# Node stages of a four-layer graph network in spans of four blocks, and the destination rows of the softmax passes summed by TensorE

## The chip, the cores and the metric

The kernel runs on one core of a Trainium2 chip. The metric is the device time of one execution in microseconds (us). The engines are named as in the profile: PE is TensorE (PEld its weight loads), DVE VectorE, ACT ScalarE, POOL GpSimd, SP SyncE, which only issues transfers here.

## The reference, cut to what matters

There are 3125 nodes with 64 features and 103125 edges sorted by destination. Four graph layers follow each other, each as `x = layernorm(x + layer(x))`.

```python
# 1: CompGCN, twice
comp = x[src] * rel_emb[l][ridx]
x = relu(agg_f @ w_fwd[l] + agg_b @ w_bwd[l] + x @ w_loop[l])
# 2: message network
msg = sum_l relu([x[src], edge] @ w1[l] + b1[l]) @ w2[l] + b2[l]
x = relu([x, segment_sum(msg) / deg] @ upd_w1 + upd_b1) @ upd_w2 + upd_b2
# 3: embedding of a time per node, then three GAT layers with 8 heads
emb = silu(pos_embed(noise_labels) @ te_w1 + te_b1) @ te_w2 + te_b2
x = x @ init_w + init_b + emb
e = exp(leaky_relu(al_s[src] + al_d[dst]) - m[dst])
x = silu(batchnorm(segment_sum(alpha * xw[src]) + gat_b + x @ adj_w + adj_b))
x = x @ out_w + out_b
# 4: attention over the edges, with K, V, Q = x @ W + b
```

## The kernel before, in words

Nodes lie in 25 blocks of 128 (NB = 25), one node per partition. Edges lie in groups of 512 of one destination block. The program is a chain of stages; between two of them every engine meets the others (`Stage.__exit__`). Two kinds of stage alternate.

**Passes over the edges** (`compgcn_pass` twice, `message_pass`, `gat_pass` three times, `attention_pass`): 114 steps of 8 tiles of 128 edges. In each step POOL issues 8 indirect transfers (L660) that gather the source rows from a table in DRAM into a ring of four buffers; it waits until the buffer of four steps ago has been used up. `pipeline` (L584) writes each engine's program as parts with lags: a few steps written out as a head, then a loop of four steps a turn, then a tail.

In `gat_pass` a step goes round PE and DVE. DVE raises the running maximum of the two destination blocks (`maxima`, L1609 to L1638) and leaves it, with the destination terms of the logits, as three bf16 parts per group in `gat_parts`. PE looks up the destination rows of the 1024 edges (`dst_gather`, L1735): eight matmuls of 48 columns, 3 parts x 16 values side by side. DVE adds the three parts (L1644, into `gat_drow`), makes the logits (L1647 to L1653), and later the messages (L1660). PE's order in a step is `turn` (L1707), `sums(0)` (L1745), `dst_gather` (L1735), `turn_back` (L1713), `sums(1)` (L1745) and `pick` (L1723); DVE's `maxima` of the next step waits for `pick`, and `turn` for the gathered rows by way of ACT (L1566).

**Stages over the nodes**: `compgcn_nodes`, `project_nodes` (tables of the message and attention passes), `message_nodes`, `diffusion_embed`, `gat_tables`, `gat_nodes`, `diffusion_out`. Each is a hardware loop, block by block or in rounds of five blocks. In most of them DVE first copies the block into a tile with a fixed address (`flat`), PE transposes it, ACT copies the transpose out of PSUM (`tall`), PE multiplies it with the weights, and DVE or ACT writes the result; one bank is used for each of these products, and PE starts a block's transposes only when ACT has emptied the bank, its products only when the copy is there. In `compgcn_nodes`:

```python
pe.wait_ge(staged, b * 2 + 2)
pe.wait_ge(evacuated, b * 2 + 1)
pe.transpose(agg_t[:, 0:P], flat[:, 0:P], m.ident[:, :])
pe.transpose(x_t[0:DIM, 0:P], flat[:, P:3 * DIM], m.ident[:, :]).then_inc(turned, 1)
pe.wait_ge(evacuated, b * 2 + 3)
```

`diffusion_embed` computes, ahead of its loop, the angles of all 3200 nodes on DVE (L1346 to L1353) and their sine on ACT (L1368), and in its loop the two products of the time network. `gat_tables` multiplies each block with weights that hold a zero column per head, and adds the ones of these columns by a matmul with one row (L1487); its table goes to DRAM block by block (L896). `gat_nodes` waits after its loop for all blocks, then runs the statistics of the batch norm on DVE (L1808, L1810), the root on ACT (L1832) and a SiLU over the whole tile on ACT (L1835). A product in f32 stands in the trace as two matmul records and two weight loads, a transpose as one.

Of the kernel before, what the change touches and what calls it, by code (L numbers as in the profile page):

```python
# [20 lines left out]
ALU = mybir.AluOpType  # L21
# [24 lines left out]
ROUND = 5  # L46
# [7 lines left out]
def build(nc, a, out):  # L54
    m = Mem()
    m.norms = 0
    with ExitStack() as ctx:
# [45 lines left out]
        with ExitStack() as c:  # L103
# [5 lines left out]
            residual_norm(nc, m, m.y)  # L109
        message_tables(nc, m, a)  # L110
        message_pass(nc, m, a)
        message_nodes(nc, m, a)
        with ExitStack() as c:
            def cb(name, shape, dt=F32):
                return c.enter_context(nc.sbuf_tensor(name, shape, dt))
            m.ft = cb("ft", [P, 2, NP])
            m.ft2 = cb("ft2", [P, 2, NP])
            m.al_d, m.top = cb("al_d", [P, NB, HEADS]), cb("top", [P, NB, HEADS])
            m.dst_parts = cb("dst_parts", [P, NB, PARTS, HEADS], BF16)
            cur, nxt = m.ft, m.ft2  # L120
# [12 lines left out]
        finish(nc, m, out)  # L133

# [449 lines left out]
def pipeline(eng, *parts, per_turn=RING):  # L584


    last = max(lag for lag, _ in parts)
    head = -(-last // per_turn) * per_turn
    whole = STEPS // per_turn * per_turn

    def at(times):
        for t in times:
            for lag, part in parts:
                if 0 <= t - lag < STEPS:
                    part(Step(None, (t - lag) // per_turn, (t - lag) % per_turn, per_turn))

    at(range(head))
    with eng.Fori(head // per_turn, whole // per_turn) as turn:
        for r in range(per_turn):
            for lag, part in parts:  # L600
                part(Step(turn, (r - lag) // per_turn, (r - lag) % per_turn, per_turn))
    at(range(whole, STEPS + last))

# [288 lines left out]
def write_table(sp, table, tile, width, stored, ahead, written):  # L892

    with sp.Fori(0, NB) as b:
        sp.wait_ge(stored, b + (1 + ahead))
        sp.dma_start(table[ds(b * P, P), :].unsqueeze(1), tile[:, ds(b, 1), 0:width]).then_inc(written, 16)  # L896
    sp.wait_ge(written, 16 * NB)


def compgcn_nodes(nc, m, a, layer, x, y):  # L900

    with Stage(nc, f"gcn_nodes{layer}") as st:
        loaded, staged, turned = st.sem("loaded"), st.sem("staged"), st.sem("turned")
        evacuated, product, stored, written = st.sem("evacuated"), st.sem("product"), st.sem("stored"), st.sem("written")
        w_agg, w_loop = st.sb("w_agg", [P, DIM]), st.sb("w_loop", [DIM, DIM])
        first = st.sb("first", [P, 1])
        flat, tall, tall_x = st.sb("flat", [P, 3 * DIM]), st.sb("tall", [P, P]), st.sb("tall_x", [DIM, P])
        agg_t, x_t, res = m.ps[0], m.ps[1], m.ps[2]
        with nc.Block() as block:
            @block.sync  # L910
            def _(sp):
# [3 lines left out]
                if layer == 0:  # L915
                    write_table(sp, m.x_table, y, DIM, stored, 1, written)

            @block.vector
            def _(dve):
                with dve.Fori(0, NB) as b:  # L920
                    dve.wait_ge(turned, b + 1)
                    dve.tensor_copy(flat[:, 0:P].unsqueeze(1), m.acc[:, ds(b, 1), 0:P]).then_inc(staged, 1)
# [1170 lines left out]
```

## Time and profile before

| | |
|---|---|
| median of 3 runs | 9469.13 us (9462.7 to 9487.42) |
| the profiled execution | 9480.35 us |
| its span | 9478.5 us |
| PE busy | 6510.8 us (69%) |
| POOL busy | 6088.3 us (64%) |
| DVE busy | 4520.1 us (48%) |
| ACT busy | 2030.6 us (21%) |
| mean granted TensorE clock | 0.655 of full speed |

Busy times are sums over stages that are bound by different things, so they are read stage by stage. The granted clock has two levels here, 0.5 (1.2 GHz) and 1.0 (2.4 GHz); a mean between them is a mix in time.

### The profile page before, as it was taken

How to read it: one execution, taken by the hardware profiler on the slowest of the kernel's cores; microseconds unless marked ns; L12 is line 12 of the kernel's file. 1: busy time of each engine (PE TensorE's matmuls, PEld its weight loads, DVE VectorE, ACT ScalarE, POOL GpSimd, SP SyncE). 2: the span in 40 equal slices, each digit the busy share in tenths (PEclk: the TensorE clock that was granted, in tenths of full speed). 3: DMA queues.
4: the chain of work that ended last, by engine and by line, in shares of the span. 5: the costliest groups of instructions: out<-in, count | busy, mean ns of one | idle time of the engine just before them, and what ended most of it. 6: DMA issues, size and time to landing. Idle time of an engine off the chain costs nothing. (4 is left out here: it accounts for less than half of the span.)

```text
span 9478.5 us, 139096 instructions
## 1 busy us (share of the span) xinstructions
PE 6510.8 (69%) x32379; PEld 5639.1 (59%) x32380; DVE 4520.1 (48%) x12932; ACT 2030.6 (21%) x5522; POOL 6088.3 (64%) x6396
## 2 busy tenths in 40 slices
PE   3556666666655556477877777777778888666766
PEld 3555556666544444346666646666667877566666
DVE  4444423333211111347777637777746666444444
ACT  2333321111122222212222212222122222211111
POOL 4777747777467777056666446666537777277776
PEclk7666555656577777567777767777755555566666
DMA  4555533333133333045555335554424444144443
GB/s 137 167 168 171 165 86 92 93 91 91 43 92 92 91 92 83 8 128 152 149 148 148 97 108 149 149 151 147 119 69 116 115 113 115 41 137 131 131 131 104
DMA packets 780185, 1092.58 MB, mean 115 GB/s; under 512 B 395392, under 2 KB 435008, under 8 KB 779728
## 3 DMA queue, kind: packets, MB, share of 16 engines
q1 hardware_dynamic: 546352, 588.70, 20.4%
q0 software_dynamic: 233760, 503.07, 20.1%
q8 instruction: 26, 0.43, 0.0%
q14 instruction: 47, 0.39, 0.0%
HBM read 1016.16 MB, written 75.04 MB: 115 GB/s over the span
## 5 line engine op out<-in xcount | busy, mean ns | idle before, releaser
L660 POOL DMA_INDIRECT gat_rows<-xw_table,gat_index x2736 | 2592.4, 948 | 1758.6 <-issue 1075.6
L1745 PE MATMUL bank<-gat_msg_s,gat_hot 128*128 128x264 f32 (+1 forms) x5472 | 1799.6, 497 | 27.2 <-DVE gat_msg_s L1660 26.5
L1745 PEld LDWEIGHTS bank<-gat_msg_s,gat_hot 128*128 128x128 f32 x5472 | 1322.7, 283 | 267.4 <-issue 32.0
L872 PE MATMUL bank<-gcn_rel,gcn_rhot 100*128 100x64 f32 x3648 | 763.3, 397 | 867.2 <-DVE gcn_rhot L827 867.0
L872 PEld LDWEIGHTS bank<-gcn_rel,gcn_rhot 100*128 100x128 f32 x3648 | 729.7, 306 | 911.3 <-issue 455.9
L660 POOL DMA_INDIRECT att_rows<-pre_table,att_index x912 | 862.8, 946 | 448.7 <-issue 276.0
L660 POOL DMA_INDIRECT msg_rows<-pre_table,msg_index x912 | 862.6, 946 | 412.7 <-issue 277.8
L660 POOL DMA_INDIRECT gcn_rows<-x_table,gcn_index x912 | 883.7, 969 | 361.5 <-issue 277.8
L660 POOL DMA_INDIRECT gcn_rows<-in_x,gcn_index x912 | 883.0, 968 | 333.9 <-issue 270.2
L1723 PEld LDWEIGHTS bank<-gat_ends_s,gat_hot 128*128 128x128 f32 x5472 | 966.7, 267 | 34.7 <-ACT gat_hot L698 2.9
L1723 PE MATMUL bank<-gat_ends_s,gat_hot 128*128 128x9 f32 x5472 | 916.8, 305 | 3.5 <-DVE gat_ends_s L1599 2.1
L709 PE MATMUL bank<-gcn_msg_s,gcn_hot 128*128 128x128 f32 x3648 | 768.6, 397 | 17.7 <-DVE acc L720 17.7
L840 DVE TENSOR_TENSOR bank<-gcn_rows,bank 128x512 f32<-128x512 f32 x228 | 158.7, 696 | 1293.0 <-DMA gcn_rows<-x_table,gcn_index 713.3
L709 PEld LDWEIGHTS bank<-gcn_msg_s,gcn_hot 128*128 128x128 f32 x3648 | 733.0, 306 | 18.8 <-issue 18.8
L709 PE MATMUL bank<-msg_msg_s,msg_hot 128*128 128x129 f32 x1824 | 394.7, 403 | 459.6 <-ACT msg_msg_s L1131 453.2
L1660 DVE TENSOR_TENSOR gat_msg_s<-gat_rows,bank 128x2112 f32<-128x2112 f32 (+1 forms) x342 | 680.8, 1991 | 0.1
L709 PEld LDWEIGHTS bank<-msg_msg_s,msg_hot 128*128 128x128 f32 x1824 | 365.3, 306 | 485.7 <-DVE acc L720 356.2
L709 PE MATMUL bank<-att_msg_s,att_hot 128*128 128x64 f32 x1824 | 384.8, 399 | 344.3 <-DVE att_msg_s L1996 340.8
L709 PEld LDWEIGHTS bank<-att_msg_s,att_hot 128*128 128x128 f32 x1824 | 366.4, 307 | 375.0 <-ACT att_hot L698 269.3
L1146 DVE TENSOR_TENSOR msg_pre_s<-msg_rows,bank 128x512 f32<-128x512 f32 x228 | 146.5, 684 | 887.3 <-DMA msg_rows<-pre_table,msg_index 879.8
L1735 PE MATMUL bank<-gat_parts,gat_dhot 128*128 128x48 bf16 x2736 | 156.4, 206 | 512.6 <-DVE gat_parts L1638 391.4
L1735 PEld LDWEIGHTS bank<-gat_parts,gat_dhot 128*128 128x128 bf16 x2736 | 125.7, 110 | 639.3 <-issue 635.4
(300 smaller groups left out, 9118.8 us busy)
## 6 DMA issues: line engine op xcount, KB each, us to landing
gcn_ids<-rel_rows SPq DMA_DIRECT2D x228, 400.0 KB
gat_hot_half<-edge_hots SPq DMA_DIRECT2D x342, 256.0 KB
gat_dhot<-dst_hots SPq DMA_DIRECT2D x342, 256.0 KB
gcn_dst<-dst_rows SPq DMA_DIRECT2D x114, 512.0 KB, 6.7
gat_rows<-xw_table,gat_index POOLq DMA_INDIRECT x2736
edge_hots<-gcn_hot_half SPq DMA_DIRECT2D x114, 256.0 KB, 2.1
dst_hots<-gcn_dhot SPq DMA_DIRECT2D x114, 256.0 KB, 3.5
gcn_hot_half<-edge_hots SPq DMA_DIRECT2D x114, 256.0 KB
```

The source lines that it names most:

```text
L660: pool.indirect_dma_start(self.rows[n.q][:, j, :], None, self.table, bass.IndirectOffsetOnAxis(ap=self.index[n.q][:, j:j + 1], axis=0))\
L709: ins = pe.matmul(place(banks, g, width), hot[:, g * GROUP + j, :], msg[:, g * GROUP + j, 0:width], start=j == 0, stop=j == GROUP - 1)
L840: dve.tensor_tensor(comp[q], g.rows[n.q][:, :, :], rel_ps[q][:, :].rearrange("p (b d) -> p b d", b=BATCH), ALU.mult)\
L872: ins = pe.matmul(rel_ps[q][:, j * DIM:(j + 1) * DIM], rhot[q][:, j * P:(j + 1) * P], rel[:, :], start=True, stop=True)
L1146: ins = dve.tensor_tensor(pre[q][:, part, :], g.rows[n.q][:, part, :], edge_ps[q][i][:, :].rearrange("p (j d) -> p j d", j=GROUP), ALU.add)
L1660: dve.tensor_tensor(msg[q][:, :, :].rearrange("p b (h e) -> p b h e", h=HEADS), rows[n.q][:, :, 0:wide].rearrange("p b (h e) -> p b h e", ...
L1723: ins = pe.matmul(pick_ps[:, j * (HEADS + 1):(j + 1) * (HEADS + 1)], hot[n.q][:, j, :], ends[q][:, j, :], start=True, stop=True)
L1735: ins = pe.matmul(row_ps[:, j * size:(j + 1) * size], dhot[n.q][:, j * P:(j + 1) * P], parts[q][:, j // GROUP, :, :].rearrange("p k h -> p ...
L1745: ins = pe.matmul(sum_ps[g][:, 0:wide], hot[n.q][:, g * GROUP + j, :], msg[q][:, g * GROUP + j, :], start=j == 0, stop=j == GROUP - 1)
```

## The change: what it does

All node stages are written out (no hardware loop) over seven spans, six of four blocks and one of one. Each span has one of two banks (and of two SBUF tiles) in turn; PE transposes span i before it multiplies span i-1 (`in_turn`), straight from `m.acc` and `x`, without `flat`. `message_nodes` does this with three lags. Tables go to DRAM span by span.

- The time network moves out of `diffusion_embed` into the head of `message_pass`, in seven chunks of 512 nodes on DVE, ACT and PE; `pipeline` takes parts with a count, and writes 12 steps out as the head, where it wrote 4. Seven loads on SP move with it, ahead of the loads of the edge attributes. The two buffers of `turn_ps` there become one.
- `gat_tables` has no zero columns and no matmul of ones (DVE writes them into `m.acc`), eight banks instead of two, and the SiLU of the layer before, span by span; `gat_nodes` takes its statistics span by span, and multiplies `adj` with 512 columns at a time.
- In `gat_pass` PE adds the three parts in PSUM: 24 matmuls of 16 columns a step. L1644 and the tile `drow` are gone; the logits read the bank, and `dst_gather` waits for `shifted` of the step before instead of `joined`.

```diff
-ROUND = 5
+SPAN = 4
+SPANS = [(b, min(SPAN, NB - b)) for b in range(0, NB, SPAN)]
+def in_turn(first, second):
+    for i in range(len(SPANS) + 1):
+        if i < len(SPANS):
+            first(i, *SPANS[i])
+        if i:
+            second(i - 1, *SPANS[i - 1])
...
 def compgcn_nodes(nc, m, a, layer, x, y):
+                def turn(i, b, size):
+                    if i >= 2:
+                        pe.wait_ge(agg_kept, i - 1)
+                        pe.wait_ge(x_kept, i - 1)
+                    for k in range(size):
+                        pe.transpose(agg_t[i % 2][:, k * P:(k + 1) * P], m.acc[:, b + k, 0:P], m.ident[:, :])
+                    for k in range(size):
+                        ins = pe.transpose(x_t[i % 2][0:DIM, k * P:(k + 1) * P], x[:, b + k, :], m.ident[:, :])
+                    ins.then_inc(turned, 1)
+                def products(i, b, size):
+                    pe.wait_ge(agg_kept, i + 1)
+                    pe.wait_ge(x_kept, i + 1)
+                    if i >= 2:
+                        pe.wait_ge(stored, i - 1)
+                    for k in range(size):
+                        out = res[i % 2][:, k * DIM:(k + 1) * DIM]
+                        pe.matmul(out, tall[i % 2][:, k * P:(k + 1) * P], w_agg[:, :], start=True, stop=False)
+                        ins = pe.matmul(out, tall_x[i % 2][:, k * P:(k + 1) * P], w_loop[:, :], start=False, stop=True)
+                    ins.then_inc(product, 1)
...
 def message_pass(nc, m, a):
+                pipeline(act, (0, g.bring_index(act)), (5, time_keep, TIMES), (4, time_hidden, TIMES), (1, keep),
+                         (2, hot.widen(act, summed, 1)), (2, rectify), (2, wave, TIMES))
+                pipeline(dve, (0, angles, TIMES), (1, preactivations), (3, adds))
+                pipeline(pe, (0, turn), (3, time_input, TIMES), (2, sums), (0, edge_products), (3, time_output, TIMES))
...
 def gat_tables(nc, m, a, layer, cur):
+                if layer:
+                    for i, span in enumerate(SPANS):
+                        activate(act, m, layer, cur, active)(i, *span)
+                for b in range(NB):
+                    keep(b)
...
-                    pe.matmul(o_ps[q][:, 0:both], m.ones[0:1, :], one[:, :], start=False, stop=True).then_inc(product, 1)
+                        if b >= DEEP:
+                            pe.wait_ge(terms, b - DEEP + 1)
+                        for k in range(kt):
+                            ins = pe.matmul(m.ps[b % DEEP][:, 0:width + 2 * HEADS], cur[:, k, b * P:(b + 1) * P], w[:, k, :],
+                                            start=k == 0, stop=k == kt - 1)
...
 def gat_pass(nc, m, layer):
-                    dve.tensor_reduce(drow[q][:, :, :], row_ps[:, 0:BATCH * PARTS * 2 * HEADS]
-                                      .rearrange("p (b k h) -> p b h k", b=BATCH, k=PARTS), AX.X, ALU.add).then_inc(joined, 1)
-                    dve.wait_ge(joined, n.total(1, 2))
-                    dve.tensor_tensor(lg[q][:, :, :], al_s[q][:, :, :], drow[q][:, :, 0:HEADS], ALU.add)\
+                    dve.tensor_tensor(lg[q][:, :, :], al_s[q][:, :, :], drow[:, :, 0:HEADS], ALU.add)\
...
-                    pe.wait_ge(joined, n.total(1, 1))
+                    pe.wait_ge(shifted, n.total(1, 1))
                     for j in range(BATCH):
-                        ins = pe.matmul(row_ps[:, j * size:(j + 1) * size], dhot[n.q][:, j * P:(j + 1) * P],
-                                        parts[q][:, j // GROUP, :, :].rearrange("p k h -> p (k h)"), start=True, stop=True)
+                        for k in range(PARTS):
+                            ins = pe.matmul(row_ps[:, j * size:(j + 1) * size], dhot[n.q][:, j * P:(j + 1) * P],
+                                            parts[q][:, j // GROUP, k, :], start=k == 0, stop=k == PARTS - 1)
...
 def gat_nodes(nc, m, a, layer, cur, nxt):
+                for i in range(1, len(SPANS)):
+                    divide(i, *SPANS[i])
+                    measure(i - 1, *SPANS[i - 1])
```

How PE's instructions stand in the loop of the first `gat_pass`, before (`gat_hot` holds the 0/1 tiles of destinations, `gat_dhot` their transposes):

```order
L1707 MATMUL bank<-ident,gat_al_s 64x128
L1745 MATMUL bank<-gat_msg_s,gat_hot 128x264 x4
L1735 MATMUL bank<-gat_parts,gat_dhot 128x48 x8
L1713 MATMUL bank<-ident,gat_run_max 128x64
L1745 MATMUL bank<-gat_msg_s,gat_hot 128x264 x4
L1723 MATMUL bank<-gat_ends_s,gat_hot 128x9 x8
```

and now:

```order
L1794 MATMUL bank<-ident,gat_al_s 64x128
L1833 MATMUL bank<-gat_msg_s,gat_hot 128x264 x4
L1823 MATMUL bank<-gat_parts,gat_dhot 128x16 x24
L1800 MATMUL bank<-ident,gat_run_max 128x64
L1833 MATMUL bank<-gat_msg_s,gat_hot 128x264 x4
```

Sixteen matmuls more stand ahead of `turn_back`, `sums(1)` and `pick`. On DVE, in the same loop, there stood before:

```order
L1638 TENSOR_TENSOR gat_parts<-gat_rest 128x2x8
L1591 REGISTER_ALU
L1592 SCALAR_TENSOR_TENSOR gat_run_max<-gat_runs,bank 64x128
L1644 TENSOR_REDUCE gat_drow<-bank 128x128
L1647 TENSOR_TENSOR gat_lg<-gat_al_s,gat_drow 128x64
```

and now:

```order
L1728 TENSOR_TENSOR gat_parts<-gat_rest 128x2x8
L1681 REGISTER_ALU
L1682 SCALAR_TENSOR_TENSOR gat_run_max<-gat_runs,bank 64x128
L1734 TENSOR_TENSOR gat_lg<-gat_al_s,bank 128x64
L1737 SCALAR_TENSOR_TENSOR gat_lg<-gat_lg 128x64
```

The reduction between the scan and the first sum is gone. ACT in one of the steps of the head of `message_pass` now (`te_hid` is the hidden layer of the time network, `rnd` and `ang` its angles):

```order
L670 ACTIVATE msg_index<-src_i 128x8
L1187 ACTIVATE ft<-bank,msg_b_in 128x512
L1183 ACTIVATE msg_te_hid<-bank,msg_te_b 128x512
L1168 ACTIVATE msg_attr_t<-bank 128x256
L718 ACTIVATE msg_hot<-msg_hot_half 128x1024
L1174 ACTIVATE msg_msg_s<-msg_pre_s 128x8x128
L1179 ACTIVATE msg_rnd<-msg_ang 128x512
```

L1187, L1183 and L1179 are new; they stand behind the copy of the gather's indices (L670), and the other four rows were there before.

## Rows read from the trace of the kernel before

**Rows 1.** The page: span, busy times by engine, and what the DMA engines moved.
```profile
span 9478.5 us, 139096 instructions
...
PE 6510.8 (69%) x32379; PEld 5639.1 (59%) x32380; DVE 4520.1 (48%) x12932; ACT 2030.6 (21%) x5522; POOL 6088.3 (64%) x6396
...
GB/s 137 167 168 171 165 86 92 93 91 91 43 92 92 91 92 83 8 128 152 149 148 148 97 108 149 149 151 147 119 69 116 115 113 115 41 137 131 131 131 104
```

**Rows 2.** The gathers of the first and the third `gat_pass`: first and last start.
```profile
L660 POOL DMA_INDIRECT gat_rows<-xw_table,gat_index x912: 943/949/991, 4103.0 to 5367.8; - x183
...
L660 POOL DMA_INDIRECT gat_rows<-xw_table,gat_index x912: 941/947/985, 6993.8 to 8133.3; - x183
```

**Rows 3.** Windows, node loops: start:end, us, busy of PE, PEld, DVE, ACT, POOL; PEclk.
```profile
1277.00:1342.50 65.50, 48.09 (x150) 31.00 (x150) 7.92 (x48) 16.26 (x75) 0.00 (x0) 0.50 0.05 12
...
2606.20:2637.90 31.70, 19.13 (x75) 15.66 (x75) 6.50 (x15) 3.76 (x10) 0.00 (x0) 0.50 0.14 42
3803.40:3879.60 76.20, 49.18 (x170) 35.07 (x170) 12.62 (x25) 12.34 (x30) 0.00 (x0) 0.50 0.00 0
3893.20:4028.30 135.10, 59.78 (x175) 40.20 (x175) 49.29 (x112) 45.41 (x52) 0.00 (x0) 0.50 0.04 13
4035.00:4097.30 62.30, 61.54 (x100) 24.98 (x100) 5.64 (x25) 10.07 (x25) 0.00 (x0) 0.50 0.15 54
5469.00:5554.40 85.40, 84.87 (x150) 41.82 (x150) 6.89 (x25) 10.10 (x25) 0.00 (x0) 0.50 0.11 39
6935.00:6988.00 53.00, 52.73 (x150) 37.49 (x150) 6.76 (x23) 7.38 (x25) 0.00 (x0) 0.50 0.11 33
8200.00:8229.70 29.70, 16.57 (x50) 12.58 (x50) 5.62 (x25) 7.42 (x24) 0.00 (x0) 0.50 0.00 0
8249.60:8288.00 38.40, 24.46 (x75) 19.93 (x75) 8.29 (x20) 3.76 (x10) 0.00 (x0) 0.50 0.11 34
5419.00:5441.70 22.70, 22.64 (x184) 21.80 (x182) 9.35 (x22) 14.42 (x47) 0.00 (x0) 0.99 0.00 0
```

**Rows 4.** Timeline of PE in `message_nodes`: start, us, instruction, and the idle time before.
```profile
3803.47 1.33 PE L1254 MATMUL bank<-ident,msg_nodes_flat 128*128 128x128 f32 x5 [12.49 <-DVE msg_nodes_flat L1239]
3805.66 2.39 PE L1266 MATMUL bank<-msg_nodes_w,msg_nodes_tall 128*128 128x64 f32 x10 [0.85 <-ACT msg_nodes_tall L1286]
...
3811.53 2.40 PE L1272 MATMUL bank<-msg_nodes_both_t,msg_nodes_w_u 128*64 128x512 f32 x4 [0.85 <-ACT msg_nodes_both_t L1290]
```

**Rows 5.** Timeline of DVE and ACT behind the loop of the first `gat_nodes`.
```profile
5442.33 3.78 DVE L1808 BATCH_NORM_STATS2 gat_nodes_stats<-ft 128x6 f32<-128x512 f32 x7 [2.20 <-ACT ft L1825]
...
5452.48 6.00 ACT L1835 ACTIVATE ft<-ft,gat_nodes_shift,gat_nodes_gain 128x3200 f32<-128x3200 f32 x2
```

**Rows 6.** Timeline of PE: the lookup at the high clock, then a step at the low one.
```profile
4701.28 0.36 PE L1735 MATMUL bank<-gat_parts,gat_dhot 128*128 128x48 bf16 x8 [3.28 <-DVE gat_parts L1638]
...
4723.11 0.48 PE L1735 MATMUL bank<-gat_parts,gat_dhot 128*128 128x48 bf16 x8 [2.70 <-DVE gat_parts L1638]
4723.52 0.69 PE L1713 MATMUL bank<-ident,gat_run_max 64*128 64x64 f32 x2
4724.14 3.89 PE L1745 MATMUL bank<-gat_msg_s,gat_hot 128*128 128x264 f32 x8
4727.81 3.42 PE L1723 MATMUL bank<-gat_ends_s,gat_hot 128*128 128x9 f32 x16
4731.09 0.40 PE L1707 MATMUL bank<-ident,gat_al_s 128*64 128x128 f32 x1
```

**Rows 7.** Groups: busy us, mean ns, idle before, releasers (L1723: first `gat_pass` alone).
```profile
L1644 DVE TENSOR_REDUCE gat_drow<-bank 128x128 f32<-128x384 f32 x342 | 190.6, 557 | 131.2 <-PE bank L1735 122.2 <-issue 8.1
L1735 PEld LDWEIGHTS bank<-gat_parts,gat_dhot 128*128 128x128 bf16 x2736 | 125.7, 110 | 639.3 <-issue 635.4
L1723 PE MATMUL bank<-gat_ends_s,gat_hot 128*128 128x9 f32 x1824 | 274.6, 288 | 1.1 <-ACT gat_hot L698 0.7 <-DVE gat_ends_s L1599 0.4
```

**Rows 8.** Timeline of PE in `attention_pass`: 24 matmuls of 64 columns, three parts each.
```profile
8907.93 1.49 PE L2040 MATMUL bank<-q_parts,att_dhot 128*128 x24
```

More of the change, by code:

```diff
@@ L584, in pipeline @@
 def pipeline(eng, *parts, per_turn=RING):
-    last = max(lag for lag, _ in parts)
-    head = -(-last // per_turn) * per_turn
+    last = max(part[0] for part in parts)
+    early = max([part[0] + part[2] for part in parts if len(part) > 2], default=0)
+    head = -(-max(last, early) // per_turn) * per_turn
     whole = STEPS // per_turn * per_turn
@@ new lines, in products @@
+                def products(i, b, size):
+                    pe.wait_ge(kept, i + 1)
+                    if i >= 2:
+                        pe.wait_ge(stored, i - 1)
+                    for k in range(size):
+                        at = k % each * width
+                        ins = pe.matmul(res[i % 2][k // each][:, at:at + width], tall[i % 2][:, k * P:(k + 1) * P], w[:, :],
+                                        start=True, stop=True)
+                    ins.then_inc(product, 1)
+                pe.wait_ge(loaded, 32 * len(parts))
@@ L1235, in _ @@
                 dve.wait_ge(rated, 2)
[L1236 to L1247 removed]
+                staged((0, join), (2, store))
@@ new lines, in turn_joined, with hide @@
+                def turn_joined(i, b, size):
+                    pe.wait_ge(joined, i + 2)
+                    if i:
+                        pe.wait_ge(joined_kept, i)
+                    for k in range(size):
+                        ins = pe.transpose(bt_ps[:, k * P:(k + 1) * P], both[:, b + k, :], m.ident[:, :])
+                    ins.then_inc(joined_t, 1)
+                def hide(i, b, size):
+                    pe.wait_ge(joined_kept, i + 1)
+                    if i >= 2:
+                        pe.wait_ge(hidden, i - 1)
+                    pe.matmul(h_ps[i % 2][0:DIM, 0:size * P], w_u1[:, :], both_t[i % 2][:, 0:size * P], start=True, stop=True)\
+                        .then_inc(hidden_ps, 1)
@@ new lines, in _, with turn, products @@
+            @block.tensor
+            def _(pe):
+                def turn(i, b, size):
+                    if i >= 2:
+                        pe.wait_ge(kept, i - 1)
+                    for k in range(size):
+                        ins = pe.transpose(t_ps[i % 2][0:DIM, k * P:(k + 1) * P], m.x[:, b + k, :], m.ident[:, :])
+                    ins.then_inc(turned, 1)
+                def products(i, b, size):
+                    pe.wait_ge(kept, i + 1)
+                    if i >= 2:
+                        pe.wait_ge(stored, i - 1)
+                    pe.matmul(o_ps[i % 2][:, 0:size * P], w_in[:, :], tall[i % 2][:, 0:size * P], start=True, stop=True)\
+                        .then_inc(product, 1)
+                pe.wait_ge(loaded, 16)
+                in_turn(turn, products)
@@ new lines, in gat_shape, with gat_columns, activate, part @@
+def gat_shape(layer):
+    return (1, 2, 2)[layer], (256, 256, 128)[layer]
+def gat_columns(layer):
+    kt, width = gat_shape(layer)
+    c = width // HEADS
+    wide = HEADS * (c + 1)
+    return kt, c, wide, wide + HEADS, wide + 2 * HEADS
+def activate(act, m, layer, cur, counted):
+    ot = gat_shape(layer - 1)[1] // P
+    def part(i, b, size):
+        for o in range(ot):
+            tile = cur[:, o, b * P:(b + size) * P]
+            ins = act.activation(tile, tile, ACT.Silu, bias=m.shift[:, o:o + 1], scale=m.gain[:, o:o + 1])
+        ins.then_inc(counted, 1)
+    return part
```

668 lines of the change are left out of this document (320 added, 348 removed).

## Prediction

> **What bounds the kernel now.** I read the page first, then the windows on each loop, then the timelines inside them. The page [rows 1] has PE at 69%, POOL at 64% and DVE at 48%: no engine is the bound everywhere, so I go stage by stage. The profiled execution took 9480.35 us, 11.2 above the median of 9469.13; the sum is made against the first and the median's number is 11 less. Differences under 0.3%, 28 us, can't be told from no change.
>
> The passes over the edges are bound in two ways. In the first `gat_pass` 912 gathers start over 1264.8 us: 1.388 us each, 11.1 us for a step of eight; in the third they take 1.251 each, 10.0 a step [rows 2]. The second is POOL's own uninterrupted pace (a gather of 0.95 and 0.30 before the next), the first is not: there the round of DVE and PE sets the step, and POOL waits for buffers.
>
> The node loops are bound by one block's round trip. Their windows add up to 577 us, counting the loop of `compgcn_nodes`, which runs twice, once [rows 3]. In `message_nodes` PE does a block's 5 transposes in 1.33 us, idles 0.85 until ACT has copied, does ten records in 2.39, idles 0.85 again, does four in 2.40 [rows 4]. PEclk is 0.50 in all of them, the low of the clock's two levels (1.2 GHz). The `gat_nodes` loop shows the other, 0.99, right behind a pass [rows 3].
>
> **Prices at the low clock**, all from [rows 4], with 0.4 taken off for filling the array (the one transpose of [rows 6] takes 0.40): a transpose (1.33−0.4)/4 = 0.23 us; a record of 64 or 128 columns (2.39−0.4)/9 = 0.22, two to a product; of the last row's 2.40, two records of 512 columns, 0.85 each, which is 0.43 per block for a product taken over four blocks.
>
> **The node stages.** With two banks and the transposes of span i ahead of the products of span i−1, DVE's and ACT's copies (at most 16.3 us busy of 65.5 in the first window) lie beside PE, and the stage becomes PE's stream over 25 blocks plus a fill:
> - `compgcn_nodes`, twice: two transposes, four records: 25×(0.46+0.88) = 33.5, plus 1, against 65.5: −31 each, −62.
> - tables of `message_pass`: 25×(0.23+0.44) = 16.8, plus 1.9, against 31.7: −13.
> - `message_nodes`: 25×(0.46+0.88+0.43) = 44.3, plus 2, against 76.2, and it starts some 3 earlier, as nothing is copied flat: −33.
> - `diffusion_embed`: angles and sine leave it. What stays is a load (I estimate 3.6) and 25×(0.23+0.43) = 16.5, plus 2: 22 against 135.1: −113.
> - `gat_tables`: PE is busy over 98% of it [rows 3] at the low clock, on 288 or 160 columns a block and the ones' matmul. One unbroken stream of that kind is what PE had before the one loop where 0.99 was granted. I take the high clock after 4 us: the first table 62.3 → 20.4 (then 3.5 MB at 171 GB/s, the page's fastest slice, bind), −42; the second 85.4 → 27, −58; the third 53 → 17, −36: −136. At the low clock it is only the matmuls left out: −35−36−27 = −98.
> - `gat_nodes`: the statistics (7 in 3.78 us, twice, [rows 5]) lie beside the loop, −8; the 6.00 of SiLU and its switch move behind the next stage's weight work, −7; a reciprocal and a shorter start, −2: −17 twice, −10 for the last, −44.
> - `diffusion_out` 29.7 → 25×0.44+1.3 = 12.3: −17.5. Tables of `attention_pass` 38.4 → 25×(0.23+0.68)+1 = 23.8: −14.5.
>
> These are −433. Unrolling costs nothing by itself: its cover is that the written-out heads of the passes run at their loops' pace.
>
> **The time network in `message_pass`.** Seven chunks on DVE, PE and ACT, one to a step. The ring of four buffers gives POOL four steps, 40 us, before a late step stops it. ACT's three new instructions stand ahead of other work, behind the copy of the indices (order, L670), so POOL is fed first. Seven loads on SP go ahead of the edge attributes. I take 2 us, up to 20 if the head of twelve steps turns into a round as in `gat_pass`. Without the ring's slack it would be the 45 to 49 us that ACT and DVE were busy in the embed window [rows 3].
>
> **The lookup in `gat_pass`.** Removed: L1644, 0.557 us on DVE's path, 342 times; DVE idled 131.2 ahead of it, 122.2 of them for the bank, which now comes ahead of the sum at L1734 instead [rows 7]. Added: eight matmuls of 48 columns become 24 of 16. Before they take 0.36 us at the high clock and 0.48 at the low [rows 6]. Bounds for the 24: below, the same pace per matmul, (0.36−0.2)/7 = 0.023, so 0.2+23×0.023 = 0.73; above, `attention_pass`, whose 24 of 64 columns take 1.49 [rows 8]. Four times the columns are streamed there, so I lean to the near end: 0.9 at the low clock and 0.75 at the high. That is +0.42 and +0.39 on PE, and `turn_back`, `sums(1)` and `pick` stand behind it. `pick` releases DVE's scan, and a step's PE work at the low clock is full (0.69+3.89+3.42 follow without a gap, [rows 6]).
>
> `pick` averages 2.41 us in that pass, between 1.85 at the high clock and 3.42 at the low (rows 6 and 7): about 36% of the steps are low. There PE is the longer side: +0.42. In the others DVE is: −0.557 and the 0.03 that a second instruction waits to start, +0.39, so −0.2 on the round from the parts to the logits. Over 228 steps of the first two passes: 228×(0.36×0.42−0.64×0.2) = +5. In the third, POOL's pace covers most: +0.07×114 = +8. With the 2 of `message_pass`: +15. The new wait (`shifted` for `joined`) holds PE until DVE has read the bank, a sum of 64 elements just behind the old reduction's place: nothing, since PE waits 3.28 for the parts ahead of each lookup anyway.
>
> **Sum:** −433+15 = −418: 9480.35−418 = 9062 for a profiled execution, **9051** on the median.
>
> **The rivals.**
> - *A, the lookup costs what attention's does.* 1.49 for 24: +1.0 at the low clock; at the high one I take 1.15, which nets +0.2 (1.15−0.36−0.59). For: same count and same 0/1 tiles as weights. Against: 8 in 0.36 [rows 6]. First two passes 228×(0.36×1.0+0.64×0.2) = 111, third 0.65×114 = 74, in place of 13: 9223. The Trainium skill ("TensorE: Matmul & The Clock Gate", section "Back-to-back issue gap") gives matmuls of up to 64 columns a floor of 25 ns, or 62 ns with hardware decode off; 24 of them would be an estimated 0.6 or 1.49 us, and the row of 8 in 0.36 disagrees with the second. Chance 0.12.
> - *B, the denser streams keep the high clock in more node stages.* What is left of their PE time after the change, some 33.5×2+17+44+16+11+23 = 178 us, would shrink by up to 79: 8970. Against: their records are transposes and narrow f32 products, PE was at 65 to 75% in these loops and never granted more than 0.50 [rows 3]. Chance 0.10.
> - *C, slower than before: each of the 24 pays its own weight load on the path.* A load at L1735 averages 110 ns from start to end [rows 7]; 24 unhidden are 2.64 us. On the low clock +2.2, less what DVE saves where it is the longer side (0.59×0.64): +1.83×342 = +626, and 9469−433+626 = 9662. Against: the same row has 125.7 us busy over 2736 loads, 46 ns each, and 8 loads and matmuls fit in 0.36. It decides the sign from 0.087 us a matmul (24 in 2.1 us). The skill's page "TensorE: Matmul & The Clock Gate", section "LDWEIGHTS (loading the stationary operand)", makes a load columns/1.2 ns, an estimated 107 ns for these 128 and 2.57 us for 24, which speaks against this change; the row of 8 in 0.36 disagrees, as 8 would take 0.86. Chance 0.03.
> - *D, the node loops gain nothing*: PE was 65 to 75% busy in them, and written-out code could stall as it is fetched. Only the embed stage, the tables' matmuls and the batch norm then move, −113−98−44+15 = −240: 9229. Chance 0.03.
>
> **How the numbers follow.** The forecast has 0.72. In it, tables at the low clock give +38, the fill of 20 in `message_pass` +18, and shorter fills with the lookup at its lower end some −35: 9015 to 9107. To leave out no more than 2 in 10, the range takes B in, down to 8950, and reaches most of the way to A, 9200. All cases but C are faster by far more than 28 us: faster 0.96, slower 0.03, same 0.01.
>
> **What would show it.** Right: embed near 22 us; `compgcn_nodes` near 35 at PEclk 0.50 and `message_nodes` near 46; PEclk near 1 in the three tables, with the first at 150 GB/s or more; gathers still at 1.251 in `message_pass` and its end no later; L1823 x24 near 0.9; gathers of the first `gat_pass` at 1.38 to 1.40, DVE idling for the bank ahead of L1734. Wrong: L1823 at 1.4 or more (A, C), gathers of the third pass above 1.30, PEclk above 0.6 in the early node stages (B), idle "issue" between PE's matmuls in the spans (D).

## The result, and the profile after

The changed kernel takes **9018.11 us** (9012.4 to 9021.1) against 9468.91 before: a ratio of **0.952, 95% interval 0.9504 to 0.9537**. The forecast was 9051, with a range of 8950 to 9200. The profiled execution's span is 9019.3, 459.2 less than before; the forecast for it was −418.

The page of the changed kernel, its span, busy times, granted clock and what the DMA engines moved (answers to [rows 1]):

```profile
span 9019.3 us, 144258 instructions
...
PE 6468.0 (72%) x37299; PEld 5691.4 (63%) x37300; DVE 4270.9 (47%) x12350; ACT 1977.4 (22%) x5277; POOL 6074.9 (67%) x6396
...
GB/s 132 168 169 172 168 117 92 91 92 92 76 77 93 91 93 92 66 156 150 152 151 150 95 160 148 148 147 148 94 114 113 116 113 113 68 132 131 132 130 104
```

The gathers of its three gat passes, first to last start ([rows 2] has the first and third of before; its second took 1264.5 us):

```profile
L680 POOL DMA_INDIRECT gat_rows<-xw_table,gat_index x912: 940/946/995, 3823.9 to 5074.3; - x183
...
L680 POOL DMA_INDIRECT gat_rows<-xw_table,gat_index x912: 940/946/957, 5184.9 to 6456.5; - x183
...
L680 POOL DMA_INDIRECT gat_rows<-xw_table,gat_index x912: 938/944/967, 6568.9 to 7711.3; - x183
```

The first starts of all passes cut the span into passes and the node stages between them. Worked out from such rows in both traces:

| stretch | before | after | change | forecast |
|---|---|---|---|---|
| between the gcn passes | 84.7 | 52.4 | −32.3 | −31 |
| gcn to message pass | 135.9 | 98.9 | −37.0 | −31−13 |
| message pass to first gat pass | 320.8 | 115.2 | −205.6 | −33−113−42 |
| first to second gat pass | 192.6 | 110.6 | −82.0 | −17−58 |
| second to third | 168.9 | 112.4 | −56.5 | −17−36 |
| third gat pass to attention | 171.8 | 137.0 | −34.8 | −10−17.5−14.5 |
| node stages together | | | −448.2 | −433 |
| the three gat passes | 3668.8 | 3664.4 | −4.4 | +13 |
| gcn, message, attention passes | | | −6.6 | +2 |

So 448 of the 459 us lie between the passes, and the passes, nine tenths of the time, moved by 0.1%. A stretch holds more than node stages: the last gather of a pass is followed by the steps that are still to be summed, and behind the third gat pass the lookup has made this part longer (further down). Where the stages went is in the windows on their loops (columns as in [rows 3]; the row of `gat_nodes` is left out), in order: the two `compgcn_nodes`, tables of the message pass, `message_nodes`, `diffusion_embed`, the three `gat_tables`, `diffusion_out`, tables of the attention pass:

```profile
1275.10:1308.60 33.50, 33.31 (x150) 27.92 (x150) 4.38 (x7) 6.28 (x14) 0.00 (x0) 0.65 0.09 20
2485.90:2527.00 41.10, 40.91 (x150) 34.05 (x150) 4.38 (x7) 6.32 (x14) 0.00 (x0) 0.50 0.00 0
2545.70:2564.60 18.90, 18.67 (x75) 14.60 (x75) 4.08 (x7) 3.81 (x7) 0.00 (x0) 0.50 0.25 71
3726.40:3760.90 34.50, 31.20 (x164) 22.10 (x164) 10.34 (x23) 11.21 (x21) 0.00 (x0) 0.84 0.00 0
3776.60:3795.50 18.90, 18.67 (x39) 7.18 (x39) 4.01 (x6) 3.81 (x7) 0.00 (x0) 0.50 0.00 0
3802.90:3817.80 14.90, 14.68 (x50) 11.37 (x50) 4.20 (x24) 9.38 (x25) 0.00 (x0) 0.80 0.49 172
5153.00:5178.50 25.50, 25.25 (x100) 20.30 (x100) 4.19 (x24) 11.80 (x30) 0.00 (x0) 0.92 0.31 110
6547.30:6563.00 15.70, 15.41 (x100) 15.20 (x100) 4.15 (x24) 10.27 (x32) 0.00 (x0) 0.81 0.31 94
...
7775.80:7786.90 11.10, 10.93 (x50) 10.74 (x50) 2.64 (x7) 2.73 (x5) 0.00 (x0) 0.50 0.00 0
7807.60:7831.70 24.10, 24.00 (x75) 18.65 (x75) 5.81 (x12) 3.81 (x7) 0.00 (x0) 0.50 0.18 55
```

PE's busy time now fills its windows to 98% and more (90% in `message_nodes`), where it filled 44% to 73% of them before, the tables of the gat passes left aside [rows 3]: the loops have become PE's stream. The three tables run at 0.80 to 0.92 of full clock instead of 0.50, and so does, unforeseen, `message_nodes` (0.84).

In the passes the lookup takes about the same at both clocks. Timeline of PE, a step at the high clock and one at the low:

```profile
4405.62 0.79 PE L1823 MATMUL bank<-gat_parts,gat_dhot 128*128 128x16 bf16 x24 [0.24 <-issue]
...
4416.16 0.77 PE L1823 MATMUL bank<-gat_parts,gat_dhot 128*128 128x16 bf16 x24 [3.25 <-DVE gat_parts L1728]
```

What DVE saved came back as waits for PE. Groups of the first gat pass after (busy us, mean ns of one, idle before), then those that answer to L1833 and L1699 in the same pass of before:

```profile
L1833 PE MATMUL bank<-gat_msg_s,gat_hot 128*128 128x264 f32 x1760 | 669.7, 545 | 6.7 <-DVE gat_msg_s L1747 6.6
...
L1810 PE MATMUL bank<-gat_ends_s,gat_hot 128*128 128x9 f32 x1778 | 293.3, 303 | 0.8 <-DVE gat_ends_s L1689 0.8
...
L1734 DVE TENSOR_TENSOR gat_lg<-gat_al_s,bank 128x64 f32<-128x64 f32 x111 | 24.5, 221 | 79.8 <-PE bank L1823 79.8
L1699 DVE TENSOR_SCALAR gat_pen<-bank 128x8 f32<-128x8 f32 x111 | 18.4, 166 | 203.7 <-PE bank L1810 161.5 <-issue 42.3
```

```profile
L1745 PE MATMUL bank<-gat_msg_s,gat_hot 128*128 128x264 f32 x1760 | 632.8, 521 | 11.4 <-DVE gat_msg_s L1660 11.0
L1609 DVE TENSOR_SCALAR gat_pen<-bank 128x8 f32<-128x8 f32 x111 | 18.5, 167 | 190.6 <-issue 118.3 <-PE bank L1723 72.3
```

DVE no longer spends 0.557 us a step on L1644, 62 us in this pass. Ahead of the logits it now idles 79.8 us for the bank, where it idled 41.3, and ahead of `maxima` 203.7 instead of 190.6, most of it for `pick` now. That is 52 of the 62 us. PE in its turn has become slower: the same 1760 records of the message sums take 37 us longer, `pick` 24.5 longer (268.8 to 293.3) and the lookup 37.8 longer (49.2 to 87.0). The sums and the picks together are 61 us over 111 steps, 0.55 a step; in the second pass it is 0.47. What makes these two slower stands in the granted clock of the first two passes, before and after:

```profile
4103.00:5368.00 1265.00, 984.91 (x4771) 808.19 (x4771) 905.70 (x2993) 276.99 (x1126) 864.08 (x912) 0.75 0.51 151
5560.00:6825.00 1265.00, 982.17 (x4758) 805.57 (x4759) 905.89 (x2993) 276.56 (x1124) 864.04 (x912) 0.75 0.51 151
```

```profile
3824.00:5074.00 1250.00, 1076.07 (x6538) 890.33 (x6538) 842.75 (x2882) 279.62 (x1122) 861.29 (x911) 0.69 0.52 152
5185.00:6456.00 1271.00, 1065.91 (x6533) 885.98 (x6534) 840.62 (x2882) 281.20 (x1123) 860.79 (x911) 0.70 0.51 150
```

### The profile page after: what moved, and what is told of

Its sections match the earlier page's. It is cut to its first block and busy times, and to the rows that moved or that the text cites. A ratio compares the mean times of both kernels' runs of the same rounds, so it can differ in the third digit from the quotient of the medians.

```text
span 9019.3 us, 144258 instructions
## 1 busy us (share of the span) xinstructions
PE 6468.0 (72%) x37299; PEld 5691.4 (63%) x37300; DVE 4270.9 (47%) x12350; ACT 1977.4 (22%) x5277; POOL 6074.9 (67%) x6396
## 5 line engine op out<-in xcount | busy, mean ns | idle before, releaser
L680 POOL DMA_INDIRECT gat_rows<-xw_table,gat_index x2736 | 2585.1, 945 | 1417.5 <-issue 1061.9
L1833 PE MATMUL bank<-gat_msg_s,gat_hot 128*128 128x264 f32 (+1 forms) x5472 | 1868.7, 512 | 10.1 <-DVE gat_msg_s L1747 9.5
L1833 PEld LDWEIGHTS bank<-gat_msg_s,gat_hot 128*128 128x128 f32 x5472 | 1369.6, 291 | 255.5 <-issue 13.8
L1810 PEld LDWEIGHTS bank<-gat_ends_s,gat_hot 128*128 128x128 f32 x5472 | 1030.4, 282 | 40.2 <-issue 3.2
L1810 PE MATMUL bank<-gat_ends_s,gat_hot 128*128 128x9 f32 x5472 | 971.8, 316 | 2.2 <-DVE gat_ends_s L1689 2.2
L1823 PEld LDWEIGHTS bank<-gat_parts,gat_dhot 128*128 128x128 bf16 x8208 | 250.3, 102 | 609.8 <-issue 606.4
L1823 PE MATMUL bank<-gat_parts,gat_dhot 128*128 128x16 bf16 x8208 | 268.8, 173 | 475.8 <-DVE gat_parts L1728 363.0
```

The lines of the kernel that those rows point to most:

```text
L680: pool.indirect_dma_start(self.rows[n.q][:, j, :], None, self.table, bass.IndirectOffsetOnAxis(ap=self.index[n.q][:, j:j + 1], axis=0))\
L1810: ins = pe.matmul(pick_ps[:, j * (HEADS + 1):(j + 1) * (HEADS + 1)], hot[n.q][:, j, :], ends[q][:, j, :], start=True, stop=True)
L1823: ins = pe.matmul(row_ps[:, j * size:(j + 1) * size], dhot[n.q][:, j * P:(j + 1) * P], parts[q][:, j // GROUP, k, :], start=k == 0, stop=k ...
L1833: ins = pe.matmul(sum_ps[g][:, 0:wide], hot[n.q][:, g * GROUP + j, :], msg[q][:, g * GROUP + j, :], start=j == 0, stop=j == GROUP - 1)
```

## The experiments

Theory: the node stages carry the whole gain, and the lookup nothing, since DVE's and PE's rounds in a gat pass are about equally long, and the clock falls when PE has more matmuls. Rivals: the lookup gains or costs by itself; one of the two rounds alone sets the step; written-out code or spans alone, not the overlap, gained in the node stages.

The first four runs fell on a chip on which the kernel before takes 12558 us; the changed kernel wasn't run there. The questions were put again on chips where the kernel before takes 9467 (e9 to e12) and 9484 (e5 to e8), so e1 to e4 are told briefly. Differences to the 9018.11 of the changed kernel are differences between chips too. Beside the changed kernel the one before took 9468.91, so 9467 can be compared with it directly, and of the differences in e5 to e8 some 7 to 10 us belong to the chip, as their ratios to the kernel before show.

**e1, the lookup alone**, put into the kernel before; and **e2, all but the lookup**, the changed kernel with the `gat_pass` of before. The edit is the `gat_pass` part of the diff above, applied to the one and taken back in the other.

> The kernel before, with the lookup of gat_pass alone as in the change (24 matmuls of 16 columns, no reduction on DVE). Theory 1 (the lookup trades about 0.35 us of PE for 0.56 us of DVE on a round in which sometimes the one and sometimes the other is longer): the three passes together move by -4, as in the trace after (-14, +7, +3), so 9455 to 9475. Theory 2 (the shorter DVE round is given back by a lower granted clock): the same time, and PEclk in the first two gat passes falls from 0.75 to about 0.69, which the change alone does not tell from an effect of the node stages. Rival (the reduction lay on the path in each step): -0.56 x 342 = -190, 9280. Rival (the lookup costs more than it saves): over 9490.

> The changed kernel with the gat_pass of before (8 matmuls of 48 columns and the reduction on DVE). Node stages and the time network stay changed. If the node stages carry the whole gain, 9010 to 9035 and a ratio to before of 0.952 to 0.954; if the lookup carried part of it, up to 9018+64 = 9080 or more. PEclk in the first two gat passes should be 0.75 again if the lookup lowered it, 0.69 if the stages ahead did.

e1: 12448.39 against 12558.42, ratio 0.9914 (0.9897 to 0.9931). e2: 12133.17, ratio 0.9663 (0.9642 to 0.9684). Here the lookup alone gains 0.9%. POOL's gathers in e1, and DVE's longest wait (in total, times, longest), show what is different on this chip:

```profile
L660 POOL DMA_INDIRECT gat_rows<-xw_table,gat_index x2736 | 2584.2, 945 | 3513.2 <-DVE gat_msg_s L1658 1989.2 <-issue 834.0 <-DVEq L1691 690.0
```

```profile
DVE gat_lg L1645 <- remote: 1944.6, 322, 7.1
```

POOL waits 3513 us in the gat passes (1417.5 in the changed kernel on the other chip), most of it for the message product that frees a buffer. One step takes 1833.2/114 = 16.1 us instead of 11.1. The expectations of e5 and e6 say that the gathers landed later here. The DMA packets in the traces don't show that: in the first gat pass the last packet of a gather ends 2.45 us (median) after the gather starts, in e9 on another chip 2.47. What is late is something ahead of the logits, behind a lookup that by its records has ended; the profile calls it only "remote", and what it is stays open.

**e3 and e4, `pick` in bf16**, with the new lookup and with that of before. The maxima picked at the ends of runs only keep the exponents small, and the same value is used everywhere. So they are rounded to bf16, and the half-width 0/1 tiles serve as weights.

```diff
-        ends = ring_sb(st, "ends_s", TWO, [P, BATCH, HEADS + 1])
+        ends = ring_sb(st, "ends_s", TWO, [P, BATCH, HEADS + 1], BF16)
...
-                    hots.wait(pe, n)
+                    pe.wait_ge(hots.hot_in[n.q], n.count(16, 16))
...
-                        ins = pe.matmul(pick_ps[...], hot[n.q][:, j, :], ends[q][:, j, :],
+                        ins = pe.matmul(pick_ps[...], hots.half[n.q][:, j, :], ends[q][:, j, :],
...
+                def load_hot(n):
+                    sp.wait_ge(picked, n.total(1, 1))
+                    hots.load(sp)(n)
```

> The changed kernel; the picked run maxima are rounded to bf16, so pick is 8 bf16 matmuls with the half-width 0/1 tiles instead of 8 f32 products (16 records, 1.85 us at the high clock and 3.42 at the low). Any value near the maximum serves, since the same value is used in every exponent. Theory P (in the first two gat passes PE is on the round that sets the step): both passes fall from 1250 and 1271 to the pace of POOL's gathers, 1142, so -237: 8780. Rival D (DVE's own round sets it): -60 or less, 8960 or more. The third pass is POOL's and does not move in either.

> As e3, but with the lookup of before (8 matmuls of 48 columns, DVE adds the three parts). If the steps are then bound by POOL's pace, the same time as e3 within 10 us, and the lookup is worth nothing in either form. If DVE's round has become the bound, 0.56 us in 228 steps shows: +100 to +130 over e3.

e3: 11973.49, ratio 0.9536 (0.9517 to 0.9556). e4: 12296.57, 0.9792 (0.9772 to 0.9812). On that chip the lookup in the bank is worth 2.6% when `pick` is in bf16 (0.9536/0.9792), and e4 is slower than e2, which differs from it only in `pick`. That last point stays open. The numbers of neither theory hold here.

**e5, all but the lookup, again.**

> The kernel of e2 once more: on the chip of e1 to e4 the gathers themselves landed later (the kernel before took 12558 us there, and POOL waited for rows in every pass), so that the round of DVE and PE was not what set the step. On a chip where the kernel before takes about 9469: 9010 to 9035 if the lookup carried nothing and the node stages all; 9080 or more if DVE's 0.56 us counted in each of the 228 steps of the first two gat passes. PEclk in these two passes back to 0.75 if the lookup lowered it to 0.69.

9040.12 (9037.3 to 9057.69), ratio 0.9533 (0.952 to 0.9546): 22 us over the changed kernel, and 5 over the 9010 to 9035 that was expected. By the ratios, 0.9533 and 0.952, it is 12 us, with intervals that overlap. In the profiled execution, the slowest of the five, the first two passes take 1273.9 and 1276.1 us, and their clock is back:

```profile
3826.00:5085.00 1259.00, 976.97 (x4679) 803.15 (x4678) 891.93 (x2950) 276.31 (x1108) 847.08 (x894) 0.74 0.51 150
5195.00:6460.00 1265.00, 981.48 (x4702) 806.77 (x4702) 881.64 (x2924) 280.40 (x1115) 835.65 (x881) 0.75 0.51 149
```

**e9, the lookup alone, again**, against the kernel before on the same chip, with 11 and 15 runs:

> The kernel of e1 once more (the kernel before, with the lookup of the change alone). From the changed kernel against e5, pass by pass: -24 in the first gat pass, -4 in the second, +2 in the third, so 9440 to 9455 beside a before of about 9470 to 9480. If the node stages ahead of a pass mattered to these (start of the pass, clock), another split between the passes. The rival that the lookup costs what I forecast: +13.

9487.95, ratio **1.002 (1.0011 to 1.0029)**: 0.2% slower, against the 9440 to 9455 that was expected. The windows of its first two passes:

```profile
4105.00:5360.00 1255.00, 1064.48 (x6526) 883.67 (x6526) 840.82 (x2874) 277.05 (x1117) 855.19 (x905) 0.70 0.51 150
5560.00:6835.00 1275.00, 1090.58 (x6644) 904.72 (x6644) 856.02 (x2926) 280.35 (x1134) 857.19 (x907) 0.70 0.50 148
```

e5 and e9 together show that it is the lookup that lowers the clock, 0.75 to 0.70, whatever the node stages are. What it is worth in time is −0.1% from the one side (e5) and +0.2% from the other (e9): nothing that counts. That the lower clock is what cancels DVE's saving fits the sums above, but no run held the clock and changed the lookup, so it isn't shown. Why the first gat pass took 1250 us in the changed kernel, in e7 and e8, and 1263 in e9 and e12, with the same code in the pass, stays open; the last two have the `diffusion_embed` of before in common.

One cost of the lookup shows in every trace. In the third gat pass, where POOL's pace of 10.0 us a step covers the round, PE is one step further behind when the last gather starts. Records of the message sums behind that moment, before, after and in e9 (count, shortest/median/longest in ns, first and last start):

```profile
L1745 PE MATMUL bank<-gat_msg_s,gat_hot x48: 434/434/596, 8136.5 to 8155.6; 128*128 128x136 f32 x48
```

```profile
L1833 PE MATMUL bank<-gat_msg_s,gat_hot x64: 431/434/593, 7713.7 to 7744.1; 128*128 128x136 f32 x64
```

```profile
L1744 PE MATMUL bank<-gat_msg_s,gat_hot x64: 434/434/594, 8127.4 to 8157.9; 128*128 128x136 f32 x64
```

Sixteen records more are left, a step's worth, and the last sum ends 33.3 us behind the last gather's start instead of 22.7. It is 33.2 in e7, e8, e9, e11 and e12, which have this lookup and the f32 `pick`, and 20 to 23 in e5 with the lookup of before and in e6 and e10 with `pick` in bf16. So 10.6 us of the lookup stand in the stretch from the third gat pass to the attention, where the table above has node stages.

**e7, spans one after the other.**

```diff
 def in_turn(first, second):
-    for i in range(len(SPANS) + 1):
-        if i < len(SPANS):
-            first(i, *SPANS[i])
-        if i:
-            second(i - 1, *SPANS[i - 1])
+    for i in range(len(SPANS)):
+        first(i, *SPANS[i])
+        second(i, *SPANS[i])
```

and in `message_nodes` all five parts of a span before the next.

> The changed kernel; in the node stages each span is finished before the next begins (no transposes of span i ahead of the products of span i-1; same spans, same banks, same written-out code). Theory 1 (the gain of the node loops is that PE no longer waits for the copies): PE idles about 1 us per copy and span, 0.85 in the rows of before but for four blocks longer, so compgcn_nodes +7, tables of the two passes +5 each, message_nodes +15 to +20, embed +5: +45 to +60 in all, of the 145 that these loops gained; the rest is what spans of four save by themselves. Rival (dense streams are granted a higher clock): the stages also fall back to PEclk 0.50, message_nodes from 29 us to 55 or more, +80 to +100. Rival (unrolling alone was the gain): under +15.

9106.54, ratio 0.9606 (0.9591 to 0.9621): +88. `compgcn_nodes` (the first) and `message_nodes`:

```profile
1277.70:1326.60 48.90, 43.20 (x150) 33.57 (x150) 4.38 (x7) 6.34 (x14) 0.00 (x0) 0.50 0.07 16
3758.60:3830.70 72.10, 51.33 (x164) 33.24 (x164) 10.22 (x23) 12.18 (x21) 0.00 (x0) 0.50 0.00 0
```

The stretches between the passes grew by 75 us, and 42 of them lie between the message pass and the first gat pass. In size this is nearer to the rival with the clock (80 to 100) than to theory 1 (45 to 60): `message_nodes` goes from 34.5 back to 72.1, of which 20 us are the same 164 records at the low clock (31.20 to 51.33 busy) and 17.5 more are idle. In the other stages the overlap is worth what theory 1 says: the second `compgcn_nodes` takes 48.7 against 41.1.

**e8, spans of one block** (`SPAN = 1`).

> The changed kernel with spans of one block instead of four: the lag and the two banks stay, a copy or a semaphore round now falls on every block. Theory 1 (PE's stream hides the copies): a block's PE time at the low clock, 1.34 us in compgcn_nodes, just covers a copy of 128 columns and its wait, so +0 to +10 in each of the stages, +30 in all, and gat_nodes +20 more, since its products take 128 columns at a time. Rival (the span size is what gained, a copy costs 1 us of round trip each): 25 instead of 7 rounds, about +18 in each of nine stages, +150.

9134.21, ratio 0.9634 (0.9619 to 0.9649): +116. The first `compgcn_nodes`, `message_nodes`, and the first table:

```profile
1277.80:1317.40 39.60, 39.37 (x150) 32.16 (x150) 7.07 (x25) 12.44 (x50) 0.00 (x0) 0.50 0.09 21
3750.00:3819.20 69.20, 63.65 (x200) 39.30 (x200) 18.75 (x77) 21.50 (x75) 0.00 (x0) 0.50 0.00 1
3868.60:3882.60 14.00, 13.79 (x50) 10.80 (x50) 4.18 (x24) 9.39 (x25) 0.00 (x0) 0.85 0.52 176
```

`compgcn_nodes` keeps its gain without spans of four, as the overlap alone hides the copies. `message_nodes` loses the clock, though PE is busy 92% of its window, and its 164 records have become 200, as each product of a span is now one of a block. The share of busy time alone doesn't tell the two states apart. The first of the tables has the high clock in e7 (0.85) and e8 as well. The stretches between the passes grew by 88 us, 43 of them between the message pass and the first gat pass; the forecast of theory 1, +50, and that of the rival, +150, both miss.

**e12, the time network back** in `diffusion_embed`, with `message_pass` and `diffusion_embed` of before.

> The changed kernel with message_pass and diffusion_embed as before: the angles, the sine and the time network are computed in diffusion_embed again, block by block. Theory (the network is hidden in the gathers' slack of message_pass, which took 1139.1 us after against 1139.5 before): +110 to +115, 9130, and message_pass stays at 1139 to 1140. Rival (it cost message_pass something that another part of the change paid back): message_pass shorter than 1139, less than +100.

9151.62, ratio 0.9663 (0.9648 to 0.9678): +133. The stretch from the message pass to the first gat pass takes 227.8 instead of 115.2, +112.6, as the theory says, and the first gat pass 12 more (the open point above). The message pass is 2 us shorter without the network, 1137.1 against 1139.0 and 1139.2 in e10 and e11 on the same chip, so there the rival is right:

```profile
L680 POOL DMA_INDIRECT msg_rows<-pre_table,msg_index x912: 940/944/957, 2571.5 to 3708.6; - x183
```

**e6, `pick` in bf16, again.**

> The kernel of e3 once more, for the same reason. PE on the round (theory P): the first two gat passes fall to POOL's pace, 1142 each, the whole to about 8780. DVE's own round sets it (rival D): 8960 or more. The third pass does not move.

**8939.58**, ratio 0.9427 (0.9412 to 0.9441): −79 (−88 by the ratios), a third of what theory P says, and less time than the 8960 or more of rival D. `pick` now takes 0.35 to 0.41 us, where it took 3.42 at the low clock [rows 6], and the two passes take 1222.5 and 1226.0. DVE's timeline shows what is late next:

```profile
4402.51 0.35 PE L1814 MATMUL bank<-gat_ends_s,gat_hot_half 128*128 128x9 bf16 x8
...
4403.49 0.43 DVE L1775 TENSOR_TENSOR acc<-acc,bank 128x264 f32 x1
...
4405.10 0.17 DVE L1703 TENSOR_SCALAR gat_pen<-bank 128x8 f32<-128x8 f32 x1 [1.19 <-issue]
```

`pick` has ended at 4402.86, DVE has nothing to wait for from 4403.92 on, and starts 1.19 us later. Between the two instructions it loads the numbers of the destination blocks into registers. Over all three gat passes these waits are 565.1 us in 337 times, 1.68 on average and 2.5 at most.

**e10 and e11, these registers loaded early**, with `pick` in bf16 and without. In three steps of four DVE loads them behind the message product (2.35 us long), ahead of the last addition.

```diff
+                def fetch(n):
+                    if n.q != TWO:
+                        first = n.turn is None and n.total(1, 0) == 0
+                        ahead[:] = blocks_of(nc, dve, m, n, 0 if first else PAIR)
...
-                    ids = blocks_of(nc, dve, m, n, 0 if first else PAIR)
+                    ids = list(ahead) or blocks_of(nc, dve, m, n, 0 if first else PAIR)
+                    ahead.clear()
...
-                pipeline(dve, ..., (3, add(0)), (2, messages), (3, add(1)))
+                pipeline(dve, ..., (3, add(0)), (2, messages), (1, fetch), (3, add(1)))
```

> e6, and DVE loads the block numbers of the next step's maxima right behind the message product, ahead of add(1), in three steps of four; nothing else moves. In e6 DVE stands 1.19 us or more ahead of L1703 (the first of maxima) waiting for nothing that the profile shows, just where these registers are loaded. Theory L (the load of the registers is on DVE's round, and with pick in bf16 this round sets the step): -1.2 in 3 of 4 steps, from 10.7 down to POOL's 10.0: the first two gat passes to 1142 to 1150, the whole 8775 to 8800. Rival (the stall is something else, or PE's round is as long): no change from e6, 8940.

> The changed kernel with the early load of e10 alone, pick stays f32. If PE's round is the longer one there, as much as DVE's or more (both theories of e6 held in part: -80 of the 237), the early load gives less than alone on DVE: 8960 to 9010. If DVE's round alone set the step, -0.9 x 228 = -200: 8820. If nothing was on that load: 9018 to 9030.

e10: **8737.63**, ratio **0.9229 (0.9215 to 0.9243)**. e11: 8871.59, ratio 0.9367 (0.9352 to 0.9381), better than the 8960 to 9010 that equal rounds were to give and short of the 8820 of DVE alone. In e10 both passes run at POOL's pace, 1138.7 us each, 1.250 a gather, as theory L says:

```profile
L680 POOL DMA_INDIRECT gat_rows<-xw_table,gat_index x912: 940/946/962, 3826.4 to 4965.1; - x183
...
L680 POOL DMA_INDIRECT gat_rows<-xw_table,gat_index x912: 942/946/994, 5066.1 to 6204.8; - x183
```

DVE's waits ahead of the first instruction of `maxima` in all gat passes (in total, times, longest), in the changed kernel and in e10:

```profile
DVE gat_pen L1699 <- PE bank L1810: 593.9, 274, 3.7
...
DVE gat_pen L1699 <- issue: 117.1, 66, 2.5
```

```profile
DVE gat_pen L1709 <- issue: 200.5, 85, 2.5
```

The 594 us for the bank of `pick` are gone, and the wait for nothing is left in one step of four. In the changed kernel most of the time is put down to the bank, and the load counts all the same: a wait is put down to the cause that ends last, and that hides the other. Over the first two passes `pick` alone gains 73 us, the early load alone 143, both 245: each frees room that the other then uses. e10 beats both kernels, and every pass of it is at POOL's pace (1137 to 1159 us).

## Why the prediction was right, step by step

- **Node stages, −433 forecast, −448 measured.** Right in kind and size. The embed loop takes 18.9, the tables 14.9, 25.5 and 15.7 (forecast 20.4, 27 and 17), and their clock is 0.80 to 0.92. Their loops gave back 144 us (by windows), so of the two sums, −136 and −98, the high clock's was right. The forecast gave each table 4 us at the low clock first; those means make it some 6, 4 and 6. The five transposes of [rows 4] are those of a round of five blocks, not of one block as the forecast says; the price of one is the same.
- **Prices.** The price of 0.22 us for any record of 64 columns was too low for `compgcn_nodes`: two products that alternate between weights of 128 and 64 rows come every 0.62 us a pair of records, 0.31 each (timeline of PE in its second run):

```profile
2490.41 0.69 PE L961 MATMUL bank<-gcn_nodes_w_agg,gcn_nodes_tall 128*128 128x64 f32 x2
2491.02 0.69 PE L962 MATMUL bank<-gcn_nodes_w_loop,gcn_nodes_tall_x 64*128 64x64 f32 x2
```

So that loop took 41.1, not 34.5. The price had come from one row of `message_nodes`; the loop's own busy time stood in [rows 3]. Whether the alternation is the reason wasn't tried. That the first run of the loop took 33.5, and its stretch −32.3 for −31, is luck: the low price and the clock that wasn't foreseen (0.65) cancel.
- **Clock.** The 0.50 forecast for the stages outside the gat layers' own held in five of seven; `message_nodes` (34.5 us at 0.84, forecast 46) and a part of the first `compgcn_nodes` (0.65) went the way of rival B. e7 and e8 show that `message_nodes` needs both the overlap and the spans of four for it. So B was no rival to the forecast but came true in a part: the clock isn't granted or refused for all stages together.
- **The time network** costs the message pass 2 us (e12), as forecast, and brings 113.
- **`gat_nodes`.** The two that are followed by a table have −82 and −56.5 with it (forecast −75 and −53). The last stretch has −34.8, not −42. `diffusion_out` gave 18.6 and the attention tables 14.3 in it, as forecast, and the 10.6 us that the lookup leaves behind the third gat pass are the rest: without them it is −45.
- **The lookup.** It costs 0.78 at either clock, not 0.9 and 0.75. Rivals A and C are out: 24 matmuls take 33 ns each, not 62 or 110. The sum +13 came out as −4 from first to last gather and +2 with what follows the last one, and between −12 and +21 by e5 and e9. But the reason that was given, a mix of steps at two clocks with a fixed share of 36% low, was incomplete: the share itself moves with the change. PE does 16 more matmuls a step, the clock falls from 0.75 to 0.70, and the sums and picks take 0.47 to 0.55 us a step longer, about what DVE saves. So that the forecast of the passes came near is in part luck. In the third pass +8 was forecast, and it was 3 in the pass and 10.6 behind it.
- **What was missed** is that DVE's own round holds a register load of 1.2 to 2.5 us, which the profile gives as "issue" ahead of L1609, 118.3 us in the first gat pass of before. The forecast of no gain in the passes was right, but they were not at a bound of the chip: 280 us lay in `pick` and in that load.

## What to carry to other kernels

When two engines hand a step to each other, shortening one of them shows only a part of what it is worth until the other is shortened too (here 73 and 143 us alone, 245 together). Try both together before giving either up, and look at the granted clock of the stretch before a saved half microsecond is booked. An idle time in front of an instruction that is put down to "issue", at the place where registers are loaded from memory, is a cost like any other. Here it could be hidden behind the longest instruction of the round.

## What the runs showed of the hardware

- A stream of 24 bf16 matmuls of 16 columns, each with its own weight load, takes 0.77 us at 1.2 GHz and 0.79 at 2.4 GHz (timeline of the changed kernel): 33 ns each at either clock.
- Sixteen more such matmuls a step lowered the granted clock of a whole pass from 0.75 to 0.70 (e9 against before, and the changed kernel against e5). Taking out the f32 picks brought it to 0.75, and with the early load too to 0.78 (windows of e6 and e10).
- PE busy for 92% of the window was granted 0.50 in `message_nodes` of e8, and 0.84 for 90% in the changed kernel. The tables of before had 0.50 for over 98%, those after 0.80 to 0.92. What makes the difference between the tables was not tried; before, half of PE's time in the first of them went to the ones' products, whose weights have one row.
- Loading the block numbers into DVE's registers left it idle for 1.68 us on average and 2.5 at most (e6).
- The kernel before took 9467 to 9484 us on two chips and 12558 on a third. There the gathers' packets landed as early (2.45 us), and a step of the first gat pass took 16.1 us instead of 11.1 (e1).
